# The setup of a graph network kernel: the row of numbers and the position masks read from PSUM in place of SBUF

## The reference

```python
# layer 0: ten steps with degrees as norms; loops = one edge of weight 1 per node
deg_out = segment_sum(w, s);  deg_in = segment_sum(w, d)
wn = w * rsqrt(deg_out)[s] * rsqrt(deg_in)[d]
h = 0.9 * segment_sum(h[s] * wn[:, None], d) + 0.1 * x      # x10
x = layernorm(x + h)
# layer 1: scores of edges, one exp of a clipped sum per head, messages summed by dst
score = exp(clip(sum(K[src] * Q[dst] / sqrt(8) * (edge_attr @ WE + bE)), -5, 5))
out = layernorm(x + segment_sum(V[src] * score, dst))
```

## Time and profile before

| | us |
|---|---|
| median of three runs | 10065.58 |
| lowest and highest run | 10062.63, 10071.41 |
| span of the profiled execution | 10063.8 |
| own time of the profiled execution | not given apart from its span |

### The profile page before, as it was taken

The page is one execution under the profiler, slowest core; times in us unless marked ns, Lnnn a source line. Parts: engine busy times, 40 slices in busy tenths (PEclk is TensorE's granted clock), DMA queues, the critical chain, the costliest instruction groups (busy, mean ns, idle before and its releaser), DMA issues.

```text
span 10063.8 us, 145017 instructions
## 1 busy us (share of the span) xinstructions
PE 8794.6 (87%) x50360; PEld 5055.3 (50%) x50360; DVE 5147.9 (51%) x14830; ACT 5554.1 (55%) x7215; POOL 7343.7 (73%) x7701
## 2 busy tenths in 40 slices
PE   5899992999999999999999999999999866666665
PEld 5899991333333333333333333333333565556665
DVE  8788881444444444444444443444434455566666
ACT  1233331777777777777777787777877511111111
POOL 5677777777777777777777777777777377777776
PEclk5555555999999999999999999999999767767677
DMA  8982322999999999999999999999989565555554
GB/s 298 388 331 72 77 70 66 345 347 311 347 312 345 348 310 349 310 346 348 309 346 311 347 346 309 348 308 348 344 310 342 181 163 144 144 144 144 143 143 119
DMA packets 1378009, 2669.57 MB, mean 265 GB/s; under 512 B 683776, under 2 KB 713379, under 8 KB 1377270
## 3 DMA queue, kind: packets, MB, share of 16 engines
q1 hardware_dynamic: 958006, 2245.72, 62.7%
q0 software_dynamic: 248000, 261.74, 10.9%
q10 hardware_dynamic: 171264, 152.74, 5.3%
HBM read 2426.96 MB, written 232.42 MB: 264 GB/s over the span
## 4 chain that ended last, share of the span: by engine, by line
PE 42%; POOL 36%; issue 13%; DVE 5%; DMA 3%; ACT 1%; SPq 0%; DVEq 0%; POOLq 0%; ACTq 0%
PE banks L2299 29%; POOL arena L1634 19%; POOL arena L1648 15%; PE banks L2268 5%; PE banks L2350 3%; DVE arena L1897 2%; PE banks L2269 2%; POOL dense L1610 2%; DVE arena L1930 1%; PE banks L2343 1%; DMA arena<-node_rows,src_idx 1%; DMA x_sb<-in_edge_weight_dram 1%; PE banks L2377 1%; ACT arena L1682 1%; DMA u_sb<-key_rows 0%
## 5 line engine op out<-in xcount | busy, mean ns | idle before, releaser
L1634 POOL DMA_INDIRECT arena<-node_rows,src_idx x4800 | 4582.1, 955 | 1581.5 <-issue 1453.7
L1703 ACT ACTIVATE arena<-arena 128x1024 f32<-128x1024 f32 x4900 | 4761.8, 1044 | 1506.4 <-DMA arena<-dense 1349.3
L2299 PE MATMUL banks<-arena,u_sb 128*64 128x512 f32 x11760 | 2610.8, 595 | 209.7 <-ACT arena L1703 209.4
L2299 PE MATMUL banks<-arena 128*64 128x512 f32 x12240 | 2714.4, 595 | 19.6 <-ACT arena L1703 19.4
L1648 POOL DMA_INDIRECT arena<-kv_rows,src_idx x1568 | 1502.2, 958 | 597.1 <-issue 477.7
L2299 PEld LDWEIGHTS banks<-arena,u_sb 128*64 128x64 f32 x11760 | 843.4, 138 | 1678.5 <-issue 1588.1
L2042 DVE TENSOR_SCALAR arena<-banks,rel,w_tab 128x128 f32<-128x128 f32 x4800 | 1604.3, 404 | 123.5 <-DVE arena L2059 97.7
L2299 PEld LDWEIGHTS banks<-arena 128*64 128x64 f32 x12240 | 880.9, 137 | 1539.7 <-issue 1459.6
L1610 POOL DMA_INDIRECT dense<-arena x1012 | 1077.2, 1064 | 359.4 <-issue 305.9
L2268 PE MATMUL banks<-arena 128*128 128x98 f32 x3136 | 1141.4, 468 | 140.8 <-ACT arena L1682 140.8
L1682 ACT ACTIVATE arena<-arena,w_tab 128x98 f32<-128x98 f32 x1568 | 461.5, 365 | 977.7 <-DVE arena L1897 970.0
(11 more groups left out here) (243 smaller groups left out, 6116.2 us busy)
## 6 DMA issues: line engine op xcount, KB each, us to landing
arena<-dense SPq DMA_DIRECT2D x3550, 512.0 KB
dense<-blank SPq DMA_DIRECT2D x5, 26112.0 KB, 190.0
arena<-in_dst_dram SPq DMA_DIRECT2D x195, 512.0 KB
arena<-node_rows,src_idx POOLq DMA_INDIRECT x4800
arena<-in_edge_attr_dram SPq DMA_DIRECT2D x195, 256.0 KB, 3.3
u_sb<-key_rows ACTq DMA_DIRECT2D x26, 1792.0 KB
dense<-blank SPq DMA_DIRECT2D x1, 44800.0 KB, 202.8
arena<-key_rows ACTq DMA_DIRECT2D x23, 1792.0 KB, 9.1
```

What stands on the lines that cost most here:

```text
L1634: gp.indirect_dma_start(out=rows_in[:, n % ROWS, s, :], out_offset=None, in_=node_rows[k % 2], in_offset=bass.IndirectOffsetOnAxis(ap=src_ ...
L1703: nc.scalar.activation(planes[:, q % PLANES, half, :], ring[:, n % SLOTS, :], ACT.Relu, scale=-1.0 if half else 1.0).then_inc(planes_act, 1)
L2299: done = mm(banks[h * D:(h + 1) * D, sum_slot(k, g), :], u, rows[:, h * 512:(h + 1) * 512], start=first, stop=last, tile_position=(0, h * ...
```

## The change

In `setup_dve`, after the digits are made and their semaphore is raised, DVE copies `iota_f` (128 columns) and `prior` (256 columns) to PSUM bank 7, and waits for the second copy. The one-hots of the degrees, the second comparison of chunk 0 and the comparisons of chunks 2 to 8 read the copies. The later copy of `iota_f` to the same place, L2007, goes away. The first comparison of chunk 0 (L1915), the comparisons of chunk 1 (L1949) and the two for the remaining repeats (L1982) read SBUF as before. PE's use of `earlier` at L2274 is as before.

```diff
         dve.sem_inc(digits_made, 1)
 
+        iota_ps = banks[:, 7, 0:P]
+        prior_ps = banks[:, 7, P:3 * P]
+        earlier_ps = banks[:, 7, 2 * P:3 * P]
+        v.tensor_copy(iota_ps, iota_f[:, :])
+        link(v.tensor_copy(prior_ps, prior[:, :]))
+
         def hots(n):
...
             def is_digit(to, digit, size):
-                return v.tensor_tensor(to, iota_f[:, 0:size].unsqueeze(1).broadcast_to([P, HB, size]), digit[:, at].unsqueeze(2).broadcast_to([P, HB, size]), ALU.is_equal)
+                return v.tensor_tensor(to, iota_ps[:, 0:size].unsqueeze(1).broadcast_to([P, HB, size]), digit[:, at].unsqueeze(2).broadcast_to([P, HB, size]), ALU.is_equal)
...
                     v.scalar_tensor_tensor(junk[:, s, 0:P], keys[:, s, e], key[:, t:t + 1], weights[:, s, e], ALU.is_equal, ALU.mult, accum_out=add_w[:, t:t + 1])
-                    last = v.scalar_tensor_tensor(junk[:, s, P:2 * P], keys[:, s, e], key[:, t:t + 1], earlier, ALU.is_equal, ALU.mult, accum_out=repeats[:, s:s + 1])
+                    last = v.scalar_tensor_tensor(junk[:, s, P:2 * P], keys[:, s, e], key[:, t:t + 1], earlier_ps, ALU.is_equal, ALU.mult, accum_out=repeats[:, s:s + 1])
...
-                    last = v.scalar_tensor_tensor(junk[:, s, 0:2 * P], keys[:, s, e], key[:, t:t + 1], prior[:, :], ALU.is_equal, ALU.mult, accum_out=same_before[:, t - SUM_TILES:t - SUM_TILES + 1])
+                    last = v.scalar_tensor_tensor(junk[:, s, 0:2 * P], keys[:, s, e], key[:, t:t + 1], prior_ps, ALU.is_equal, ALU.mult, accum_out=same_before[:, t - SUM_TILES:t - SUM_TILES + 1])
...
         v.tensor_copy(out_scale[:, :], inv_out[:, :])
-        v.tensor_copy(banks[:, 7, 0:P], iota_f[:, :])
         v.tensor_copy(banks[:, 7, P:P + 1], blank[:, 0:1])
```

## The result

| | before | after |
|---|---|---|
| median of four runs each, same chip, us | 10064.69 | 9981.47 |
| lowest to highest | 10062.63 to 10071.41 | 9977.97 to 9985.44 |
| ratio, 95% interval | | 0.9916 (0.9904 to 0.9928) |
| span of the profiled execution | 10063.8 | 9976.1 |
| `flag`, the end of the setup | 1732.57 | 1643.80 |

The changed kernel is 83 us faster, 0.84%; the forecast was 9980. In two later groups of runs the kernel before takes 10068 and 10071 us, and variants that keep the whole change 9986. The forecast did not cover that.

A forecast was written before the change was run, and what follows sets the result against it. The prediction took POOL's queue of scatter DMAs to end the setup, the only part touched. Its terms, 81.5 + 4 = 85.5 us, off the 10065.6 us median gave 9980 us; range 9970 to 9990, chance 0.70.

The forecast's parts named there:

- What bounds the setup: End of the setup: POOL's queue of 1088 scatter DMAs ends it, not PE, though PE looks busiest.
- What the scatters wait for: Setup: POOL's DMAs wait for DVE instructions reading two SBUF tensors, 1071 ns against 968 when DVE is quiet.
- rival 1: Setup comparisons with a mask still count as two SBUF inputs through their scalar column; about 10010 us, chance 0.20.
- rival 2: Setup scatters: no change, the excess comes from DVE's writes or from ACT and PE; 10066 us, chance 0.05.
- Middle, 81.5 us: Setup, 440 to 1535 us: 791 DMAs each 103 ns shorter, all on the path, 81.5 us gained.
- 290 to 440 us, 4 us: Setup: 81 plain writes, one DMA in four in the chain in the first 16 rounds; 4 us, bounds 0 and 10.2.
- 80 to 290 us, 0: Setup: 76 accumulating DMAs; an earlier end likely waits for the first group's clearing; 0 taken, bounds 0 and 7.8 us.
- DVE's durations, no difference: Setup comparisons and one-hots: DVE takes the same time with one operand in PSUM, 688 beside 685 ns.
- What is late next: Setup's middle: POOL issues 861 DMAs, stands at 1018 at 1535 us, 70 behind DVE, which does not become the limit.
- Rival 1's price: Setup scatters' excess: one-hots' share 66% by count times duration squared, 57 us of 85.5, giving 10009 us.
- Rival 3, slower: Setup: PSUM operands lengthen each comparison until DVE ends the setup; 10108 us at 200 ns more each, chance 0.03.

The follow-up runs named there:

- e6: Changed kernel with three in four of the in-degree matmuls left out; 9983.28 us on the first kind of chip.
- e1 again: Changed kernel with both masks back in SBUF, only the one-hots' row of numbers read from PSUM; 9990.43 us, ratio 0.9921 to the kernel before.
- e3: Changed kernel with the scale of the 6272-element multiplication copied to PSUM first; 12697.44 us, ratio 1.0157 to the kernel before, second kind of chip.
- e4: Changed kernel with an added 1024-element SBUF-to-SBUF DVE copy ahead of each folded round; 12742.63 us (one run), second kind of chip.
- e5: Changed kernel with a DVE probe before the first round, comparisons and one-hots with an operand in turn in SBUF and PSUM; 10024.5 us.
- g2: Changed kernel with six already satisfied waits on POOL ahead of each folded scatter; 9985.6 us, first kind of chip.
- p1: Changed kernel with a one-column POOL memset ahead of each folded scatter; 9985.91 us, ratio 0.9916 to the kernel before.
- g1: Changed kernel with POOL's folded scatters held back until the last one-hots are used; 11093.07 us, first kind of chip.

## Why the prediction was right, and where it was not

- **What bounds the setup: right** on the first kind of chip. e6 takes away a third of PE's work and nothing is gained; in e1 again the end moves later as POOL's scatters grow.
- **What the scatters wait for: right for the kernel, too narrow as a rule.** 1071 ns became 969 (forecast 965 to 975), with a scalar column still in SBUF: it doesn't count, so rival 1's condition is refuted. So is rival 2: PE, ACT and DVE's writes are as before, and the excess is gone. e3 shows it on a single instruction, 0.95 to 1.01 us for 7.47. The Trainium skill's inference in "SBUF — State Buffer", "Who interferes with whom", that descriptor generation isn't held by a tensor_tensor, would have left 1071 ns; the runs decide against it. But e4's copy, one tensor, holds scatters too.
- **Middle, 81.5 us: 78.3** between the same two scatters. The 791 scatters took 81.2 us less (847.3 to 766.1), and the idle time between them grew by 2.8.
- **290 to 440 us, 4 us: 6.5.** More than one DMA in four was in the chain.
- **80 to 290 us, 0: 5.8.** The step that failed. It laid the gap of 11 us to the clearing of the first group; it was the landing of POOL's own last accumulating DMAs, which moves with them, and the 76 DMAs became 5.8 us shorter in sum (125.9 to 120.1). The two early terms are 12.3 for 4 us, the middle 3.2 us less than forecast, and the last 140 scatters, which the sum left out, cost 1.9 us: the setup is 3.3 us better than the sum. On the medians the gain is 83.2 us, 2.3 below the sum, within the spread of the runs. That the time came out within 1.5 us is in part luck, as the misses cancel.
- **DVE's durations, no difference: right**, by a hair on the good side (681 for 685, 476 for 484). In "VectorE: DVE Perf Modes" the skill has 62 cycles more for a PSUM source; e5's pairs, 2.50 and 2.48 us for four, show nothing of it.
- **What is late next: right.** POOL stayed 77 to 86 scatters behind DVE in the middle. At 1535 us it stood at 1018, as forecast, but from 166 + 852 and not from 157 + 861: the misses cancel here too. PE's last setup matmul ends at 1538 us. The 6.5 us DMA stayed.
- **Rival 1's price: wrong.** It split the excess by count and the square of the duration, 66 to 34. Measured, it is about 90 to 10, on both kinds of chip. In the trace of before, scatters that start during a one-hot carry 190 ns of excess each, those that start during a comparison 49. Each comparison is followed by a read of its accumulator (84 ns); that this frees the scatter sooner fits, but was not tried.
- **Rival 3, slower: wrong in its mechanism, and yet slower happened elsewhere.** No comparison grew. On the second kind of chip DVE and PE, with late signals between them, are what ends the setup, and the change costs 1.8%. No row of the profile before showed such a wait, so neither the range nor the chances held it. Why the late signals cost the changed kernel more stays open: DVE's PSUM reads and POOL's denser scatters would both fit. Six waits or a memset can't space the scatters out (g2, p1); holding them all back (g1) would tell, but no run shows it on such a chip.

## What to carry to other kernels

Where POOL issues indirect DMAs back to back beside DVE, compare their mean duration with that in a quiet stretch; if they differ, look at which DVE instructions run when a long one starts, and move one operand of the most frequent long instructions to PSUM. The largest kind gives nearly all: here one row of 128 numbers was worth 9/10 of the gain. Don't count tensors alone: a copy of one tensor within SBUF held the scatters as well (e4). Before such a change is taken as a gain, see it on several chips: which engine ends a stretch can differ between them, with every instruction as long as before.

## What was not expected of the hardware

- Five groups of runs met two kinds of chip: the kernel before takes 10065 to 10071 us in three groups and 12478 to 12501 in two. In the setup the granted clock is 0.50 on both kinds, and what differs is signals from PE that DVE waits up to 41 us for. Behind the setup the kernel before takes 10385 us there and 8331 on the first kind, at a mean granted clock of 0.84 and 0.91; that part, which the change doesn't touch, was not looked into.
- A copy of one fp32 tensor within SBUF, 1024 elements in 0.68 us, holds up a scatter that starts in it (0.22 us in the mean; 1.42 us for 0.97 when it starts 0.1 us behind the copy).
- DVE took 4 and 8 ns less for a one-hot and a comparison with one operand in PSUM.
- The 0.30 us between two indirect DMAs on POOL hides a memset of 117 ns, and six met waits cost about 2 ns.
